# The first stage of a four-layer graph kernel: normalization folded into the ScalarE pass, eight transposition banks, and remainders placed among the DVE's other work

## The reference

```
h = maximum(layernorm(x), 0); x = x + attention(h, adj)        # layer 0, 8 heads
h = maximum(layernorm(x), 0); x = x + diffusion(h, adj, ...)   # layer 1, two steps
h = maximum(layernorm(x), 0); x = x + gcn(h, adj, W, b)        # layer 2
h = maximum(layernorm(x), 0); x = x + relu(gcn2(h, adj))       # layer 3
# layernorm(x) = (x - mean(x)) / sqrt(var(x) + 1e-5), over the 256 features
```

## Time and profile before

| what | value |
|---|---|
| median of 3 runs | 3665.94 us (3665.34 to 3668.64) |
| profiled execution, its own time | 3668.13 us |
| span of its trace | 3666.1 us |
| mean granted TensorE clock | 0.931 of full |
| busy share: PE, DVE, ACT, POOL | 80%, 64%, 34%, 1% |
| setup phase | from 0 to about 70 us of the span |

### The profile page before, as it was taken

How to read it: one execution, slowest core, us unless ns; L and a number is a source line. 1 busy time by engine, 2 the same in 40 slices (tenths; PEclk the granted TensorE clock), 3 DMA queues, 4 the chain that set the end, 5 groups by cost and what they waited for, 6 DMA issues and landing times. The chain is left out here.

```text
span 3666.1 us, 57967 instructions
## 1 busy us (share of the span) xinstructions
PE 2938.1 (80%) x20312; PEld 2140.7 (58%) x20312; DVE 2347.9 (64%) x4563; ACT 1252.7 (34%) x1676; POOL 50.0 (1%) x69
## 2 busy tenths in 40 slices
PE   1449999999999999999998566884774677775499
PEld 1236676766667676676765254663453465664388
DVE  7975555555565555556564698889588969684330
ACT  3433434344334443443433223332214434311211
POOL 0000000000000000000000100000000000000110
PEclk9989999999999999999999788997887888997699
DMA  5764848567483866838486110110010010100400
GB/s 190 292 235 117 201 99 199 126 172 189 110 197 97 200 144 152 202 95 197 106 190 163 40 58 12 58 47 1 21 35 24 12 35 12 35 24 21 194 1 24
DMA packets 585578, 396.80 MB, mean 108 GB/s; under 512 B 538339, under 2 KB 550630, under 8 KB 559846
## 3 DMA queue, kind: packets, MB, share of 16 engines
q1 hardware_dynamic: 583430, 380.47, 38.8%
q10 hardware_dynamic: 2016, 14.68, 1.0%
HBM read 223.06 MB, written 37.81 MB: 71 GB/s over the span
## 5 line engine op out<-in xcount | busy, mean ns | idle before, releaser
L667 DVE SCALAR_TENSOR_TENSOR e_lo<-e,e_hi 128x2048 f16<-128x2048 f32 x128 | 293.3, 2291 | 456.9 <-ACT e_hi L595 456.9
L549 PE MATMUL av<-vw_hi,pT_hi 128*128 128x256 f16 x2048 | 559.6, 273 | 7.5 <-DMA pT_lo<-e_lo 7.5
L549 PE MATMUL av<-vw_lo,pT_hi 128*128 128x256 f16 x2048 | 559.6, 273 | 0.0
L549 PE MATMUL av<-vw_hi,pT_lo 128*128 128x256 f16 x2048 | 559.6, 273 | 0.0
L538 PE MATMUL logits<-kT_hi,qT_hi 128*128 128x512 f16 x1024 | 389.1, 380 | 7.2 <-DVE att_small L653 5.5
L1741 DVE SCALAR_TENSOR_TENSOR nuc_junk<-nuc_e,nuc_thr 128x2048 bf16<-128x2048 f32 x168 | 388.4, 2349 | 5.1 <-issue 0.4
L538 PE MATMUL logits<-kT_hi,qT_lo 128*128 128x512 f16 x1024 | 388.2, 379 | 0.0
L538 PE MATMUL logits<-kT_lo,qT_hi 128*128 128x512 f16 x1024 | 388.2, 379 | 0.0
L589 ACT ACTIVATE att_small<-att_small,minus 128x1 f32<-128x1 f32 x128 | 37.7, 294 | 828.8 <-DVE att_small L662 828.8
L590 ACT ACTIVATE e<-e,att_small,sc 128x2048 f32<-128x2048 f32 x128 | 266.1, 2079 | 0.0
L595 ACT ACTIVATE e_hi<-e 128x2048 f16<-128x2048 f32 x128 | 244.6, 1911 | 15.3
(11 more groups left out here) (397 smaller groups left out, 5883.8 us busy)
## 6 DMA issues: line engine op xcount, KB each, us to landing
bias<-bias_scratch SPq DMA_DIRECT2D x130, 1028.0 KB, 4.8
bias_scratch<-adj_bias SPq DMA_DIRECT2D x16, 1028.0 KB, 3.9
adjT_scratch<-adjT SPq DMA_DIRECT2D x16, 1024.0 KB, 7.0
nuc_at_hi<-adjT_scratch SPq DMA_DIRECT2D x32, 512.0 KB, 3.9
nuc_at_lo<-adjT_scratch SPq DMA_DIRECT2D x32, 512.0 KB, 4.8
adjT<-adjT_scratch SPq DMA_DIRECT2D x16, 1024.0 KB, 21.0
adj_rows<-in_adj_dram ACTq DMA_DIRECT2D x14, 1024.0 KB, 8.5
hx<-in_x_dram SPq DMA_DIRECT2D x1, 2048.0 KB, 8.5
```

Source lines behind the costliest of these rows:

```text
L549: last = nc.tensor.matmul(AV[par][:, :], PT[par][w][:, m, :], VW[x][:, m, :], start=(m == 0 and w == x == 0), stop=(m == T - 1 and w == 1))
L667: nc.vector.scalar_tensor_tensor(out=EL[:, :], in0=E[par][:, :], scalar=P_SCALE, in1=EH[:, :], op0=ALU.mult, op1=ALU.subtract).then_inc(lo ...
```

## The change

Four things are changed in `setup`, and nothing elsewhere.

- The 16 DVE instructions that centre and scale `hx` are gone. In their place DVE multiplies `rstd` with 16 (`H_SCALE`) and forms `minus = -mean * rstd`, two instructions on 128 by 16 values. ACT's 16 rectifying passes now compute `relu(rstd * x + minus)` with one scale and one bias for each row.
- The transposed `h` has eight PSUM banks in place of two. PE no longer waits for a remainder, and starts each group when its four tiles are rectified instead of waiting for all 16.
- ACT copies the eight banks to `hT_hi` ahead of the weight parts `WH`, no longer behind them.
- DVE's eight remainders `hT_lo` move from the end: three stand behind the weight maxima (ahead of the wait for `am`), five behind the scales (ahead of the weight remainders).

```diff
-        tp = [ps(c, f"h_tp{n}", [P, BANK]) for n in range(2)]
+        tp = [ps(c, f"h_tp{n}", [P, BANK]) for n in range(8)]
 # vector
                 v.wait_ge(rstd_done, 1)
                 v.wait_ge(stats_done, 1)
-                for t in range(T):
-                    nc.vector.tensor_scalar(hx[:, t, :], hx[:, t, :], mv[:, t, 0:1], rstd[:, t:t + 1],
-                                            ALU.subtract, ALU.mult).then_inc(centred, 1)
+                link(nc.vector.tensor_scalar(rstd[:, :], rstd[:, :], H_SCALE, None, ALU.mult))
+                nc.vector.scalar_tensor_tensor(out=minus[:, :], in0=mv[:, :, 0], scalar=-1.0, in1=rstd[:, :],
+                                               op0=ALU.mult, op1=ALU.mult).then_inc(aimed, 1)
+                for n in range(4):
+                    extreme(n)
                 link.wait()
                 nc.vector.tensor_scalar(ext[:, 0:4], ext[:, 4:8], 1e-30, None, ALU.max).then_inc(extremes, 1)
+                for b in range(3):
+                    remainder(b)
                 v.wait_ge(largest, 1)
...
                 v.wait_ge(powers, 1)
+                for b in range(3, 8):
+                    remainder(b)
                 for n in range(3):
                     v.wait_ge(w_hi, n + 1)
                     link(nc.vector.scalar_tensor_tensor(out=WL[n][:, :, :], ...
-                for b in range(2 * T // 4):
-                    ...                                  # the eight remainders, after WL
 # scalar
+                s.wait_ge(aimed, 1)
                 for t in range(T):
-                    s.wait_ge(centred, t + 1)
-                    nc.scalar.activation(hx[:, t, :], hx[:, t, :], ACT.Relu, scale=H_SCALE).then_inc(rectified, 1)
+                    nc.scalar.activation(hx[:, t, :], hx[:, t, :], ACT.Relu, bias=minus[:, t:t + 1], scale=rstd[:, t:t + 1]).then_inc(rectified, 1)
+                for b in range(2 * T // 4):
+                    k, t0 = b % KC, b // KC * BANK
+                    s.wait_ge(h_tp, b + 1)
+                    nc.scalar.activation(hT_hi[:, k, t0:t0 + BANK], tp[b][:, :], ACT.Copy).then_inc(h_hi, 1)
                 s.wait_ge(powers, 1)
                 for n in range(3):
                     nc.scalar.activation(WH[n][:, :, :], stage[n][:, :, :], ACT.Copy, scale=winv[:, n:n + 1]).then_inc(w_hi, 1)
 # tensor
-                pe.wait_ge(rectified, T)
                 for b in range(2 * T // 4):
                     k, t0 = b % KC, b // KC * 4
-                    if b >= 2:
-                        pe.wait_ge(h_lo, b - 1)
+                    pe.wait_ge(rectified, t0 + 4)
                     for t in range(4):
-                        last = nc.tensor.transpose(tp[b % 2][:, ...
+                        last = nc.tensor.transpose(tp[b][:, ...
```

More of the change, by code:

```diff
@@ L187, in setup @@
     extremes, largest, powers, w_hi, stats_done = sem("extremes"), sem("largest"), sem("powers"), sem("w_hi"), sem("stats_done")
-    rstd_done, centred, rectified, h_tp, h_hi, h_lo = (sem(s) for s in ("rstd_done", "centred", "rectified", "h_tp", "h_hi", "h_lo"))
+    rstd_done, aimed, rectified, h_tp, h_hi, h_lo = (sem(s) for s in ("rstd_done", "aimed", "rectified", "h_tp", "h_hi", "h_lo"))
     ident_made = sem("ident_made")
@@ L193, in setup @@
         stats, mv = sb(c, "stats", [P, T, 6]), sb(c, "mv", [P, T, 2])
-        rstd = sb(c, "rstd", [P, T])
+        rstd, minus = sb(c, "rstd", [P, T]), sb(c, "minus_mean", [P, T])
         ext = sb(c, "ext", [P, 8])
         wo = acc
-        tp = [ps(c, f"h_tp{n}", [P, BANK]) for n in range(2)]
+        tp = [ps(c, f"h_tp{n}", [P, BANK]) for n in range(8)]
         block = nc.Block()
@@ L232, in _, with extreme @@
                 nc.vector.memset(ext[:, :], 0.0).then_inc(stats_done, 1)
-                v.wait_ge(rstd_done, 1)
-                v.wait_ge(stats_done, 1)
-                for t in range(T):
-                    nc.vector.tensor_scalar(hx[:, t, :], hx[:, t, :], mv[:, t, 0:1], rstd[:, t:t + 1],
-                                            ALU.subtract, ALU.mult).then_inc(centred, 1)
-                for n in range(4):
+                def extreme(n):
                     v.wait_ge(w_loaded[n], 16)
@@ L241, in _, with remainder @@
                     link.note(nc.vector.tensor_reduce(ext[:, 4 + n:5 + n], w, mybir.AxisListType.XY, ALU.max, apply_absolute_value=True))
+                def remainder(b):
+                    k, t0 = b % KC, b // KC * BANK
+                    v.wait_ge(h_hi, b + 1)
+                    nc.vector.tensor_tensor(hT_lo[:, k, t0:t0 + BANK], tp[b][:, :], hT_hi[:, k, t0:t0 + BANK],
+                                            ALU.subtract).then_inc(h_lo, 1)
+                v.wait_ge(rstd_done, 1)
+                v.wait_ge(stats_done, 1)
+                link(nc.vector.tensor_scalar(rstd[:, :], rstd[:, :], H_SCALE, None, ALU.mult))
[3 more added lines that the diff above has]
+                    extreme(n)
                 link.wait()
                 nc.vector.tensor_scalar(ext[:, 0:4], ext[:, 4:8], 1e-30, None, ALU.max).then_inc(extremes, 1)
+                for b in range(3):
+                    remainder(b)
                 v.wait_ge(largest, 1)
@@ L259, in _ @@
                                                         in1=WH[n][:, :, :], op0=ALU.mult, op1=ALU.subtract))
+            @block.scalar
+            def _(s):
+                s.wait_ge(aimed, 1)
+                for t in range(T):
+                    nc.scalar.activation(hx[:, t, :], hx[:, t, :], ACT.Relu, bias=minus[:, t:t + 1], scale=rstd[:, t:t + 1]).then_inc(rectified, 1)
                 for b in range(2 * T // 4):
                     k, t0 = b % KC, b // KC * BANK
[L262 to L268, removed]
-                    s.wait_ge(centred, t + 1)
-                    nc.scalar.activation(hx[:, t, :], hx[:, t, :], ACT.Relu, scale=H_SCALE).then_inc(rectified, 1)
+                    s.wait_ge(h_tp, b + 1)
+                    nc.scalar.activation(hT_hi[:, k, t0:t0 + BANK], tp[b][:, :], ACT.Copy).then_inc(h_hi, 1)
                 s.wait_ge(powers, 1)
@@ L273, in _ @@
                     nc.scalar.activation(WH[n][:, :, :], stage[n][:, :, :], ACT.Copy, scale=winv[:, n:n + 1]).then_inc(w_hi, 1)
-                for b in range(2 * T // 4):
-                    k, t0 = b % KC, b // KC * BANK
-                    s.wait_ge(h_tp, b + 1)
-                    nc.scalar.activation(hT_hi[:, k, t0:t0 + BANK], tp[b % 2][:, :], ACT.Copy).then_inc(h_hi, 1)
             @block.tensor
@@ L281, in _ @@
                 pe.wait_ge(ident_made, 1)
-                pe.wait_ge(rectified, T)
                 for b in range(2 * T // 4):
                     k, t0 = b % KC, b // KC * 4
-                    if b >= 2:
-                        pe.wait_ge(h_lo, b - 1)
+                    pe.wait_ge(rectified, t0 + 4)
                     for t in range(4):
-                        last = nc.tensor.transpose(tp[b % 2][:, t * P:(t + 1) * P], hx[:, t0 + t, k * P:(k + 1) * P], ident[:, :])
+                        last = nc.tensor.transpose(tp[b][:, t * P:(t + 1) * P], hx[:, t0 + t, k * P:(k + 1) * P], ident[:, :])
                     last.then_inc(h_tp, 1)
```

## The result

The changed kernel takes **3613.03 us** (median of 4 runs, 3611.85 to 3615.3) against 3666.72 us of the kernel before (4 runs): a ratio of 0.9852, 95% interval 0.9837 to 0.9866, so 53.7 us less. The forecast was 3653.4 us, with a range from 3650.5 to 3657.5. The direction was right, the size was not: more than four times the forecast 12.5 us was gained.

A forecast was written before the change was run, and what follows sets the result against it. DVE's instruction list and holes were taken to bound the first 70 us; centring 4.8, `am` wait 0.6, hole 2.8 and tail 4.4 gave 12.5 us off the 3665.94 us median: 3653.4 us, range 3650.5 to 3657.5.

The forecast's parts named there:

- What bounds the kernel: Setup phase, 0 to about 70 us: DVE's instruction list plus its holes sets the time; DVE's end moves 69.65 to 57.11.
- Centring: Setup, DVE after `rstd`: two small operations replace 16 instructions; first maximum 0.37 us after `rstd`, gain 4.8 us.
- ScalarE's pass: Setup, 16 rectifying passes with scale and bias: 0.50 us each (0.33 to 0.70), hidden behind DVE's maxima.
- Remainders: Setup, DVE: three before `am`, five after the scales, 0.60 us pitch (high bound 0.69); the old tail yields 4.4 us.
- `am`: Setup, DVE's wait for POOL's reduction over partitions: gone behind three remainders, 0.57 us gained.
- POOL's reduction: Rival in setup: three DVE remainders lock the reduction out, delaying `am` by 0.57 to 0.74 us; 3654.1 us, chance 0.07.
- The stage's end: End of setup: DVE's last weight remainder ends at 57.1 us, next phase's first DVE instruction at 58.0 instead of 70.54.
- later phases give part of it back: Rival after setup: TensorE's granted clock falls otherwise, costing 5 to 7 us (3659 us) or adding to the gain; chance 0.10.
- Slower: Rival in the attention phase: mean granted TensorE clock falls 1.1%, giving about 3674 us; chance 0.03.
- Something in front of DVE: Rival in setup: late loads or slow rectifying passes make DVE wait; 3658.6 us if the gain falls to 7.3; chance 0.05.

The follow-up runs named there:

- the forced repair: The changed kernel with the tie-repair question for the third row group in layer 1's first diffusion step always answered yes; 3654.51 us, ratio 0.9968.
- the new numbers in the old order: The kernel before with only the centring replaced by two small DVE operations and ScalarE's scale and bias; two banks, remainders last; 3621.61 us, ratio 0.9878.

## Why the prediction was wrong

**What bounds the kernel.** Right for the first stage: DVE's list and its holes set it, and 12.56 us came off its end.

**Each term of the sum.** Centring: the first maximum starts 0.30 us after `rstd` (0.37 forecast). ScalarE's pass: a pitch of 0.50 us (0.50); this agreement is partly luck, since the 0.33 us in it was DVE's pace and not ScalarE's, and no run shows ScalarE's own pace without the two operands. Remainders: three in 1.88 and five in 3.08 us, at a pitch of 0.60. `am`: no wait, so POOL's reduction, begun at 37.27, was not held up until the three remainders beside it ended; `am` is read at 38.84, right behind them. The Trainium skill ("SBUF — State Buffer", section "SBUF: two separate sides") lets a DVE operation and a GpSimd operation shut each other out if the former has two inputs in SBUF or runs in a two-port mode. The remainder has one input in PSUM, and the trace agrees. The stage's end: 57.98 (58.0), but by two small errors that cancel: DVE ended 0.24 us earlier than forecast, and the next phase started 1.11 us after that end, where 0.89 had been taken from the kernel before. This part is shown by the trace, and its price in the whole kernel by the forced repair, 3654.51 us.

**The step that failed** is the sentence under "What bounds the kernel now": "each microsecond off DVE's end is one off the kernel, if no other engine becomes last and no later phase gives it back". It takes for granted that all later phases execute the same instructions, merely 12.5 us earlier: the sum has no term for work that the later phases gain or lose, which puts it at nothing without a reason. That held for all but one branch. The change doesn't only move work, it also changes how `h` comes out, and some 2400 us later an exact comparison of sums takes or leaves 40.4 us of work on the engine that bounds that stretch. The two kernels that differ from their parents in this branch alone are 40.8 us (3654.51 against the changed kernel's 3613.67, measured on another chip) and 38.8 us apart; the two in which only the computation of `h` differs, 45.5 us (3659.15 against 3613.67, of which 4.9 is the centring in the first stage) and 44.6 us (5.5 of it in the first stage). The traces say it most evenly: the first step of layer 1 takes 555.9 to 556.2 us in the four profiles with 20 masked sums, and 515.3 to 515.6 us in the five with 16, in either order of the first stage. Why exactly this rounding tips exactly the third group was not looked into row by row.

The forecast should have had two peaks: about 3653 us with the repair and about 3613 without. The trace held the price: the branch's body lies between 2460.56 and 2501.28 us, entered once where five places ask. The rival "later phases give part of it back" did look at later phases, but only at TensorE's clock, not at what they execute.

**The rivals.** Slower didn't come: the attention phase, from its first DVE instruction to layer 1, takes 1823.5 us in the changed kernel and 1825.2 before. Something in front of DVE didn't come either: the banks were 5.6 us early, `Wout` was there. Of the gain, later phases gave back 0.5 us. The clock's role is in the last section; it is small.

**The remainder of the account.** By medians 53.7 us: 12.6 in the first stage, 40.4 in the branch, and 1.7 in the attention phase, less 0.5 lost in the adjacency phase, make 54.2; the spans differ by 54.4.

## What to carry to other kernels

An edit that changes the order or the fusion of floating-point operations is not only a change of timing where the program branches on data: list the branches downstream, price each body from the trace, and forecast a value for each outcome. Compare the counts of instructions of both traces by group before any theory about clocks or contention: 20 against 16 named the place at once. To value the edit itself, hold the branch fixed on both sides; here that split a gain of 53.7 us into some 12 to 14 us that the edit itself is worth (11.7 with the repair on both sides, 13.7 with it on neither) and 40 that another rounding took back, and other inputs may.

## What the runs showed of the hardware

**A granted clock of 1.00 ahead of the first recorded change says nothing.** The prediction took the earlier trace rows as transpositions at the 2.4 GHz level and held them against the Trainium skill. That was wrong. What one transposition takes (ns at least, median, at most) shows the level that it ran at. The rows are those of the kernel before, then of the changed kernel up to 24.6 us, from 25.6 us on, and of the next phase's transpositions between 70 and 75 us:

```profile
L288 PE MATMUL h_tp<-ident,hx x32: 417/421/476, 25.2 to 67.9; 128*128 128x128 f32 x32
L295 PE MATMUL h_tp<-ident,hx x12: 421/421/474, 21.9 to 24.4; 128*128 128x128 f32 x12
L295 PE MATMUL h_tp<-ident,hx x16: 272/273/328, 25.7 to 28.5; 128*128 128x128 f32 x16
L351 PE MATMUL adj_tp<-ident,adj_rows x16: 417/421/479, 70.3 to 74.6; 128*128 128x128 f32 x16
```

The busy time by stretch of the changed kernel (granted clock third from the right):

```profile
0.00:20.00 20.00, 0.00 (x0) 0.00 (x0) 7.28 (x36) 1.62 (x2) 3.99 (x9) 1.00 0.93 354
20.00:40.00 20.00, 5.68 (x32) 4.66 (x32) 19.79 (x15) 12.23 (x25) 0.40 (x1) 0.79 0.54 181
40.00:60.00 20.00, 0.00 (x0) 0.00 (x0) 17.15 (x17) 10.15 (x3) 0.00 (x0) 0.50 0.34 106
70.00:75.00 5.00, 4.44 (x16) 2.87 (x16) 4.89 (x12) 1.79 (x3) 0.00 (x0) 0.50 0.14 56
```

A transposition of 421 ns thus belongs to a granted clock of 0.50 (70 to 75 us), and one of 273 ns to 1.00. From start to start that is 0.21 us against 0.11. All 32 transpositions before have the longer time, under a shown clock of 1.00, and so do the first 12 of the changed kernel; its pace changes at about 24.9 us, within its second group of eight. So the transpositions before ran at 1.2 GHz throughout, and the 1.00 shown there was no measurement. The Trainium skill ("TensorE: Matmul & The Clock Gate", section "What's actually happening") has the array slow after idling and fast once it has been busy. Both traces agree with it, against what the prediction said.

That the clock now rises within the stage is not shown to come from the new order: with the new numbers in the old order, the last eight transpositions ran at the fast pace too.

```profile
L288 PE MATMUL h_tp<-ident,hx x8: 272/273/330, 61.3 to 62.5; 128*128 128x128 f32 x8
```

And when the changed kernel was profiled again, the first 22 were still slow (421 ns). It makes no difference to the time here, since DVE's maxima hide all of them.

**The attention phase's entry.** At the phase's start PE works at the 1.2 GHz level for a few microseconds. The busy time by stretch, before and then after:

```profile
255.00:260.00 5.00, 5.00 (x25) 3.50 (x25) 1.70 (x7) 1.21 (x2) 0.00 (x0) 0.50 0.88 325
260.00:265.00 5.00, 5.00 (x44) 4.36 (x43) 2.08 (x3) 2.24 (x4) 0.00 (x0) 0.93 0.53 205
```

```profile
242.00:247.00 5.00, 4.29 (x22) 3.10 (x23) 1.76 (x11) 1.21 (x2) 0.00 (x0) 0.53 0.72 263
247.00:252.00 5.00, 5.00 (x49) 4.49 (x47) 2.28 (x4) 2.28 (x4) 0.00 (x0) 1.00 0.67 266
```

It rises some 6 us after the phase's start (254.3 us) before, and some 4.5 us after it (242.2 us) in the changed kernel. A second low stretch follows some 48 us after the phase's start, and it too is shorter in the changed kernel. Before, then after:

```profile
301.00:309.00 8.00, 5.12 (x27) 3.76 (x28) 1.98 (x3) 2.95 (x4) 0.00 (x0) 0.57 0.49 121
290.00:298.00 8.00, 6.72 (x45) 4.92 (x46) 3.13 (x5) 2.11 (x4) 0.00 (x0) 0.79 0.36 68
```

A clock of 0.57 over 8 us means that 3.4 us of full-speed clock are missing, one of 0.79 means 1.7. Three profiles with the old order took 1825.2 to 1825.3 us for the phase, six with the new order 1822.0 to 1823.7. That the two orders part so evenly, by some 2 us, was not expected. The two low stretches together make up for about 2.7 us of full-speed clock (1.7 in the second, some 1 us at the entry), enough for it, but no run tests that they are the cause, and why they are shorter is left open.
